# A two-layer transformer with routed experts: which engine splits the first layer's expert weights, and when

## The reference

```python
x = L0_attn_hidden_states                      # 4 batches x 512 tokens x 256
xn = layernorm(x)
x = x + attn0(xn) + ffn0(xn)
xn = layernorm(x)
x = x + attn1(xn) + ffn1(xn)

# attn0: one head of width 256, softmax(q k^T / 16) v, then w_out
# ffn0:  16 experts of width 176, each token goes to its top 4:
#        sum over e of weight[t, e] * (silu(x w_gate[e]) * (x w_up[e])) w_down[e],
#        plus one shared expert of width 352
# attn1: 32 heads of width 8 in 8 groups; ffn1: 7 experts of width 256, top 3, plus a shared one
```

## Time and profile before

| | before |
|---|---|
| median of three runs | 1142.29 us |
| the profiled execution | 1137.68 us |
| its span, first to last instruction | 1135.9 us |
| TensorE matmul busy | 1009.3 us (89%) |
| VectorE busy | 758.9 us (67%) |
| ScalarE busy | 592.8 us (52%) |
| GpSimd busy | 318.2 us (28%) |
| chain that ended last, by engine | PE 65%, DVE 15%, POOL 7%, ACT 5%, issue 4%, DMA 3% |

### The profile page before, as it was taken

One profiled execution on the slowest core, in us unless ns is written; L12 is line 12 of the kernel. 1 busy time (PEld: TensorE's weight loads), 2 busy tenths in 40 slices (PEclk: granted clock), 3 DMA queues, 4 the chain that ended last, 5 costly groups with the idle time before them and its releaser, 6 DMA issues.

```text
span 1135.9 us, 17330 instructions
## 1 busy us (share of the span) xinstructions
PE 1009.3 (89%) x5716; PEld 738.8 (65%) x5716; DVE 758.9 (67%) x1575; ACT 592.8 (52%) x895; POOL 318.2 (28%) x331
## 2 busy tenths in 40 slices
PE   4999995769999846799999999999999987999995
PEld 3877874669999814555554555555555565888884
DVE  6577553466665446799888888888888846444437
ACT  6325553265565543365655666566555655444431
POOL 2005777065654510000000122222221000455442
PEclk9999998789999958899999999999999998999999
DMA  6863333364434272011111222222222124333253
GB/s 223 326 270 116 127 107 118 104 198 144 135 127 135 95 310 36 12 30 29 29 29 29 43 55 58 56 56 56 56 57 43 63 72 156 108 107 101 91 198 137
DMA packets 49139, 120.48 MB, mean 106 GB/s; under 512 B 7752, under 2 KB 24904, under 8 KB 48520
## 3 DMA queue, kind: packets, MB, share of 16 engines
q1 hardware_dynamic: 36096, 82.80, 25.2%
q0 software_dynamic: 11808, 32.37, 7.5%
q10 hardware_dynamic: 1152, 4.19, 0.9%
HBM read 72.30 MB, written 52.42 MB: 110 GB/s over the span
## 4 chain that ended last, share of the span: by engine, by line
PE 65%; DVE 15%; POOL 7%; ACT 5%; issue 4%; DMA 3%; SPq 0%; ACTq 0%; DVEq 0%; POOLq 0%
PE psum L817 10%; PE psum L839 10%; PE psum L826 8%; POOL xg L466 5%; PE psum L633 5%; PE psum L634 4%; PE psum L635 4%; DVE work_f L1709 4%; PE psum L547 3%; PE psum L549 3%; PE psum L548 3%; PE psum L619 3%; PE psum L644 2%; ACT work_f L1206 1%; PE psum L665 1%
## 5 line engine op out<-in xcount | busy, mean ns | idle before, releaser
L1709 DVE TENSOR_REDUCE work_f<-psum 128x1 f32<-128x512 f32 x512 | 335.0, 685 | 51.2 <-PE psum L817 49.8
L1206 ACT ACTIVATE work_f<-psum 128x1024 f32<-128x1024 f32 x172 | 169.0, 1023 | 112.0 <-PE psum L826 110.4
L817 PE MATMUL psum<-work_r 128*128 128x512 f32 x512 | 205.2, 440 | 19.5 <-DVE work_f L1709 6.5
L473 POOL DMA_INDIRECT yk<-yb,dest x134 | 131.4, 980 | 238.7 <-ACT yb L1059 215.0
L817 PEld LDWEIGHTS psum<-work_r 128*128 128x128 f32 x512 | 94.2, 190 | 131.3 <-DVE work_f L1709 75.5
L826 PE MATMUL psum<-qm,work_r 128*128 128x512 f32 x512 | 161.9, 398 | 4.2 <-ACT work_f L1206 2.7
L466 POOL DMA_INDIRECT xg<-xn,slot x112 | 108.4, 968 | 180.5 <-PE psum L855 142.8
L826 PEld LDWEIGHTS psum<-qm,work_r 128*128 128x128 f32 x512 | 93.6, 188 | 31.8 <-ACT work_f L1206 10.9
L1206 ACT ACTIVATE pt<-psum 128x1024 f32<-128x1024 f32 x84 | 82.9, 1023 | 50.2 <-PE psum L826 49.3
L633 PE MATMUL psum<-wexp,xbh 128*128 x268 | 102.5, 382 | 6.9 <-issue 6.8
L634 PE MATMUL psum<-wexp,xbh 128*128 x268 | 96.6, 360 | 0.0
(11 more groups left out here) (218 smaller groups left out, 2034.9 us busy)
## 6 DMA issues: line engine op xcount, KB each, us to landing
xb<-xg SPq DMA_DIRECT2D x67, 258.0 KB
xg<-in_pad SPq DMA_DIRECT2D x1, 10320.0 KB
yg<-yk SPq DMA_DIRECT2D x20, 512.0 KB, 9.4
stage<-in_moe SPq DMA_DIRECT2D x16, 608.0 KB, 4.8
xg<-in_pad SPq DMA_DIRECT2D x1, 7224.0 KB
work_r<-work_r SPq DMA_DIRECT2D x128, 48.0 KB
work_r<-work_r SPq DMA_DIRECT2D x32, 192.0 KB
stage<-in_moe SPq DMA_DIRECT2D x16, 384.0 KB, 3.8
```

Source lines behind the costliest of these rows:

```text
L473: nc.gpsimd.indirect_dma_start(yk[l], bass.IndirectOffsetOnAxis(ap=dest[:, j % 8, i:i + 1], axis=0), yb[l][:, j % 2, i, :], None).then_inc ...
L817: nc.tensor.matmul(next_bank(pe, ("scores", n), b_mx, n + 1), qs[g % 2][:, t * P:(t + 1) * P], km[g % 4][:, r, :], start=True, stop=True). ...
L1206: nc.scalar.activation(pt[((b * NG + g) * QT + t) % 3][:, 2 * h:2 * h + 2, :], psum[:, 3 + 2 * h:5 + 2 * h, :], ACT.Exp, scale=float(HD) * ...
L1709: v.reduce_max(mx[:, s % 2, i:i + 1], ring["scores", n], AX.X).then_inc(b_mx, 1)
```

## The change

Four things are moved; nothing is added to or taken from what is computed.

- **Low parts.** Experts 2, 3 and 4 go from GpSimd (between scatters) to VectorE; expert 10 goes from VectorE to GpSimd. On VectorE, expert 2 is split in batch 1 of the attention, 3 and 4 in batch 2 between the probabilities' and the context's low parts, 5 at the end of batch 2; 6 and 7 in batch 3 between the probabilities' and the context's low parts, 8 behind the context's. On GpSimd, the two pieces of expert 1 move from before the 23rd and 29th scatter to before the 25th and 31st.
- **High parts.** Experts 7 and 8 are split on ScalarE behind the copies of batch 3's probabilities; before, 7 stood in front of these copies and 8 in pair 1. Experts 9 and 10 move into pair 0, and 11 to 15 follow one in each pair.
- **Low parts within the pairs.** On VectorE 12 to 15 come in pairs 3 to 6, one each; on GpSimd 9 and 10 stand in front of the first results and 11 behind them.
- **Loads.** Nine instead of eight expert loads stand in front of the wait for the dispatch, 9 to 11 behind the first two fetches, and 12 to 15 one each behind the fetches of pairs 3 to 6.

```diff
-        BY_DVE = (5, 6, 7, 8, 10, 12, 14, 15)
+        BY_DVE = (2, 3, 4, 5, 6, 7, 8, 12, 13, 14, 15)
...
@@ SyncE @@
-            for e in range(8):
+            for e in range(9):
                 load_expert(e)
             sp.wait_ge(m_scat, scattered(0, 16 * TT * TOP0))
             load_pair(0, 0)
             load_pair(0, 1)
-            for e in range(8, 11):
+            for e in range(9, 12):
                 load_expert(e)
-            more = {3: (11,), 4: (12,), 5: (13, 14), 6: (15,)}
+            more = {3: (12,), 4: (13,), 5: (14,), 6: (15,)}
...
@@ GpSimd @@
-            first_piece = {6: 0, 22: 1, 34: 2, 46: 3, 56: 4}
-            second_piece = {12: 0, 28: 1, 40: 2, 51: 3, 60: 4}
+            first_piece = {6: 0, 24: 1}
+            second_piece = {12: 0, 30: 1}
...
             low_expert(9)
-            more = {0: (11,), 1: (13,)}
+            low_expert(10)
+            more = {0: (11,)}
...
@@ ScalarE, attention0 @@
                 if not last:
                     projections(b + 1, 4)
-                else:
-                    high_expert(7)
                 for t in range(QT):
                     act.wait_ge(a_pt, b * QT + (t + 1))
                     copy(p_hi[:, :, t * P:(t + 1) * P], ...).then_inc(a_ph, 1)
                 if not last:
                     values_projected(b + 1, 2)
+                else:
+                    high_expert(7)
+                    high_expert(8)
...
@@ ScalarE, more_experts @@
-                for e in {1: (8, 9), 2: (10, 11), 3: (12, 13), 4: (14, 15)}.get(j, ()):
+                for e in {0: (9, 10), 1: (11,), 2: (12,), 3: (13,), 4: (14,), 5: (15,)}.get(j, ()):
...
@@ VectorE, attention0 @@
-                if last:
-                    low_expert(5)
-                    low_expert(6)
-                    low_expert(7)
+                for e in {1: (2,), 2: (3, 4), 3: (6, 7)}.get(b, ()):
+                    low_expert(e)
                 for c in range(KH):
                     dve.wait_ge(a_ch, b * 2 + (c + 1))
                     v.tensor_tensor(c_lo[:, c, :], ...).then_inc(a_cl, 1)
                 if not last:
                     values_by_key0(b + 1)
+                for e in {2: (5,), 3: (8,)}.get(b, ()):
+                    low_expert(e)
                 dve.wait_ge(a_o, b + 1)
                 add_to_tokens(bass.ts(b, QT), 2).then_inc(a_y, 1)
...
@@ VectorE, more_experts @@
-                for e in {1: (8,), 2: (10,), 3: (12,), 4: (14, 15)}.get(j, ()):
+                for e in {3: (12,), 4: (13,), 5: (14,), 6: (15,)}.get(j, ()):
```

## The result

| | before | after |
|---|---|---|
| median | 1142.77 us (1142.21 to 1143.52, 4 runs) | 1159.3 us (1156.18 to 1162.18, 4 runs) |
| ratio, 95% interval | | 1.0147 [1.0116, 1.0177] |
| the profiled execution (span) | 1137.68 us (1135.9) | 1156.18 us (1154.4) |
| TensorE busy | 1009.3 us | 1014.8 us |
| GpSimd busy | 318.2 us | 307.6 us |

The account below looks back on a forecast made before the run. It took late expert loads, tied to GpSimd's dispatch, to hold up the attention near 190 us. Gains of 15.2 us there and 5.8 us among the routed pairs, 21.0 us off the 1142.29 median, gave 1121.3 us; range 1116 to 1130.

Parts of the forecast that it names:

- By itself this is worth nothing: GpSimd's dispatch: losing low parts 2 to 4 ends the last scatter 8.0 us earlier, which alone gains nothing.
- my rivals: Half clock (0.2), dispatch as bound (0.07), pair waits changing place (0.1), load wait moving to batch 2 (0.05), slower (0.03).
- 197.5: End of the attention: predicted time in us of the last addition to `x`, instead of 212.7.
- The dispatch: GpSimd's scatters: the last would end at 188.3 instead of 196.3, staying ahead of the attention.
- The port shared by VectorE and GpSimd: Dispatch beside VectorE's low parts: 0.64 us lost for each of four, ending at 190.9, still costing nothing.
- the strong form of the rule: GpSimd shut out for each whole VectorE low part: 6.0 us on the dispatch, 2.6 us on the end; chance 0.07.
- The loads and the last batch: ScalarE's 6.26 us load wait goes; the last context starts at 187.3 instead of 199.86, at full clock.
- the 15 us: Attention: the last addition to `x` comes 15.2 us earlier, or 12.5 us at half clock.
- The routed pairs: Pairs 0 to 7: gate 7 comes +41.7 us behind the addition to `x` instead of +47.5, 5.8 us earlier.
- The term for pair 6: Routed pairs: low part 11 delays load 14 and pair 6's fetch, landing at +28.3, wanted at +26.3; 2.0 us.
- my sum: Gate 7 behind the addition to `x`: 8.5 + 7 x 3.99 + 5.3 us of waits = +41.7.
- the waits only change place: Rival on the routed pairs: no gain there, 15.2 us alone, 1127.1 us, or 1129.8 with half clock; chance 0.1.

Follow-up runs that it names:

- e4: The kernel before, unchanged, run and traced a second time; 1146.8 us, one run.
- e11: The changed kernel with GpSimd's dispatch broken after every fourth scatter, by pieces of low parts 0 and 1 or subtractions of zero; 1130.6 us, ratio 0.9892.
- e13: The kernel of e12 with its six subtractions of zero on 32 columns instead of 256; 1141.5 us, ratio 0.9957.
- e5: The changed kernel, but VectorE begins the attention only when all 64 scatters have landed, expert 1's low part behind them; 1207.3 us, one run.
- e7: The changed kernel with low parts 2 to 4 back on GpSimd between scatters, and expert 11's on VectorE in pair 2; 1130.4 us, ratio 0.9884.
- e12: The kernel of e11 with expert 11's low part on VectorE in pair 2 instead of on GpSimd; 1124.2 us, ratio 0.9841.
- e9: The kernel of e7 with each of GpSimd's five low parts cut into five pieces of 256 or 240 columns at five places; 1132.6 us, ratio 0.9899.

## Why the prediction was wrong

- **The step that failed is the first sentence on GpSimd:** "By itself this is worth nothing", of the low parts that GpSimd loses. I had looked for what they cost and not for what they did: between the scatters they were the breaks in which TensorE's signals kept up. Without them batches 1 and 2 took 16.9 and 14.3 us more than the 26.15 us I gave them; with 2.5 us more in batch 0 and 1.4 us of a later start that makes 35.1 us, and 35.0 lie between 197.5 and 232.46. The 2.5 us of batch 0 are not of this step: its breaks had hardly changed, and the kernel before took longer for it in e4. Against e4 batches 1 and 2 lost 12.6 and 12.4 us. None of my rivals had this.
- **Behind it stands the trace I trusted.** I took 26.15 us per batch from an execution that had no late signal, and saw the hint only as a difference of 4.6 us between it and the median. In e4 the same kernel took 29.9 and 30.4 us for these batches. The timed runs (1142.2 to 1143.5 us there, 1138.8 to 1148.9 beside the experiments) suggest that they are late in most executions; only these two are in a trace.
- **The dispatch** began 1.4 us later and ended 7.7 us earlier relative to that (189.06 + 0.96 = 190.0; 188.3 predicted, by 8.0 us): right.
- **The port shared by VectorE and GpSimd** hardly touched the scatters. In e11, where all seven low parts of VectorE fell beside the dispatch, four scatters next to them took 1.05 to 1.08 us instead of 0.96: 0.1 us each, not the 0.64 I had taken from the routed pairs, and nothing like a whole low part. For the scatters the strong form of the rule is refuted here. For GpSimd's subtractions it is not: e13's short one, 0.26 us when alone, takes 1.05 us beside VectorE's low parts and ends just behind one of them:

```profile
175.48 1.15 DVE L1650 TENSOR_TENSOR wexp<-stage,wexp 128x960 fp32r<-128x960 f32 x1
```

```profile
175.66 1.05 POOL L507 TENSOR_TENSOR wexp<-wexp,zero 128x32 fp32r<-128x32 f32 x1
```

- **The loads and the last batch** went as predicted once the scatters were over: no wait for a load on ScalarE, two idles of TensorE of 1.66 and 1.74 us (1.7 estimated), a granted clock of 1.00, 10.3 us for the context (10.17), low part 5 just clear of the output (VectorE still idled 0.16 us before that). e11 confirms the 15 us (198.1 against 212.7); the last batch's 19.2 us in e5 and 19.5 in e11, 30.1 before, are 11 of them.
- **The routed pairs** gained 0.9 us, not 5.8. The term for pair 6 was too small: low part 11 ended at +25.2 (+23.8 predicted), the fetch went out at +25.7, took 4.76 us and landed at +30.4 (+28.3 predicted). TensorE idled 2.83 us for it, and the granted clock was 0.50 from 262.7 to 269.5, which my sum had put at nothing: gates 4 and 5 came 9.85 us apart, where 3.99 + 2.0 were predicted. My sum doesn't agree with itself either: seven periods and the 1.0 us in front of gate 2 put that gate at +17.4, and not at the +15.5 from which I took the waits behind it; it came at +16.7. So "the waits only change place", to which I gave 0.1, is nearly what happened. With that one wait removed (e7) gate 7 stands at +40.7, 1.0 us above the +39.7 that my sum makes without that term.

## What to carry to other kernels

Before work is taken from an engine because it "delays" something off the critical path, ask what its pauses give to the others. Read more than one execution of the kernel before, above all when the profiled one is faster than every timed run. And when an engine idles and the chain names "issue" or an unknown queue, compare the recorded end of its producer with its own start: a late signal shows there and in no busy time.

## What the runs showed of the hardware that was not expected

- While GpSimd issues indirect scatters back to back (one per 1.27 us), signals of TensorE come late, by up to 14.3 us, and arrive in bursts: the updates for the four projections in the changed kernel, whose matmuls are recorded 1.4 us apart and ending by 183.0, stand 0.08 us apart from 193.05 on, after the last scatter. The scatters' own signal is not held up like that: at 169.41, while the signal of batch 1's output was outstanding, GpSimd went on 0.5 us behind the last packet of its 48th scatter. Four scatters and a break in 5.6 us (e12) left batch 2 at 26.6 us, in 5.2 us (e13) it took 42.8; a limit that holds for other patterns is not shown.
- A break helps although scatters are still on their way (e9), so it is not that everything must have landed. What the signals share with the scatters is not shown. One trace differs from the rest in another way too: that of before records all 1024 increments of the scatters' semaphore, the changed kernel's 278 and e4's 329. But e12's trace records 433 of them, and its signals were nearly in time, so missing records don't tell late signals. Whether the recording of signals takes part in holding them up stays open: every run here has a granted clock on record, so none is known to have gone without it. So does why the execution of before that I read was spared.
